# A fused two-layer kernel: the second layer's experts with the shared blocks first, biases selected by TensorE, and pairs combined behind the last block

## The reference

```
scores = softmax(x @ gate_w.T)                      # 8 experts
idx = top_k(scores + gate_b, 2);  weights = scores at idx
h1 = x @ w1.T + b1;  h3 = x @ w3.T + b3             # of an expert
a  = swiglu(h1 * h3)      # g*sigmoid(1.702 g)*(l+1), g even, l odd columns, clipped at 7
y  = a @ w2.T + b2
out = sum of weights * y over the token's 2 experts + the same for one shared expert
```

## Time and profile before

| | |
|---|---|
| median of 3 runs | 1788.88 us (1788.12 to 1789.9) |
| the profiled execution | 1786.69 us, span 1784.9 us |
| busy in the span | PE 1429.1, DVE 1327.3, ACT 909.5, POOL 617.2 us |
| in 1603.8 to 1730.7 us (routed blocks) | PE 122.66, DVE 111.14, ACT 88.70 of 126.90 us |

### The profile page before, as it was taken

The page is one execution under the profiler, slowest core; times in us unless marked ns, Lnnn a source line. Parts: engine busy times, 40 slices in busy tenths (PEclk is TensorE's granted clock), DMA queues, the critical chain, the costliest instruction groups (busy, mean ns, idle before and its releaser), DMA issues. The chain is left out here.

```text
span 1784.9 us, 41566 instructions
## 1 busy us (share of the span) xinstructions
PE 1429.1 (80%) x15014; PEld 979.8 (55%) x15014; DVE 1327.3 (74%) x3609; ACT 909.5 (51%) x2099; POOL 617.2 (35%) x586
## 2 busy tenths in 40 slices
PE   1267767776749758999999999999999983779990
PEld 0167767766744324555555555555555553658870
DVE  5699999999577855666676666667667667658886
ACT  1455555555321023666666666666666651336760
POOL 3396667665012232611111111111111003275346
PEclk7678888888859969999999999999999996689995
DMA  1310000000000001211111111111111000028962
GB/s 72 98 38 2 1 1 1 1 1 1 7 6 1 10 10 20 42 27 26 26 29 31 30 30 31 30 31 29 29 31 32 8 10 14 11 95 229 249 176 88
DMA packets 146373, 71.53 MB, mean 40 GB/s; under 512 B 95219, under 2 KB 131589, under 8 KB 146053
## 3 DMA queue, kind: packets, MB, share of 16 engines
q1 hardware_dynamic: 141508, 60.62, 15.3%
q0 software_dynamic: 4096, 8.40, 1.6%
q10 hardware_dynamic: 576, 0.07, 0.0%
HBM read 38.11 MB, written 18.35 MB: 32 GB/s over the span
## 5 line engine op out<-in xcount | busy, mean ns | idle before, releaser
L1178 DVE TENSOR_REDUCE ntop<-score 128x1 f32<-128x512 f32 x512 | 318.0, 683 | 253.0 <-PE score L1059 253.0
L1137 ACT ACTIVATE prob<-score,ntop 128x512 f32<-128x512 f32 x512 | 317.6, 687 | 270.1 <-DVE ntop L1178 270.1
L391 ACT ACTIVATE hist<-zp 128x168 f32<-128x168 f32 (+1 forms) x768 | 224.1, 313 | 171.3 <-DVE zp L359 170.6
L1095 PE MATMUL turned<-ident,prob 128*128 128x128 f32 x2048 | 268.6, 280 | 1.4 <-DVE probT L1121 1.4
L441 PEld LDWEIGHTS py<-hist,diagC 128*128 128x128 f32 x2048 | 260.3, 212 | 0.0
L441 PE MATMUL py<-hist,diagC 128*128 128x128 f32 x2048 | 260.0, 295 | 0.0
L1059 PE MATMUL score<-ks,qs 64*128 64x512 f32 x1024 | 257.2, 621 | 0.0
L1095 PEld LDWEIGHTS turned<-ident,prob 128*128 128x128 f32 x2048 | 218.9, 141 | 49.2 <-issue 28.5
L411 POOL TENSOR_TENSOR xb<-xc,Bm 128x1024 f32<-128x1024 f32 x128 | 244.7, 1948 | 1.3
L354 DVE TENSOR_TENSOR gp<-hist,Ap 128x168 f32<-128x168 f32 (+1 forms) x768 | 231.0, 331 | 14.6 <-POOL xb L411 14.6
L359 DVE TENSOR_TENSOR zp<-gp,xb 128x168 f32<-128x168 f32 (+1 forms) x768 | 234.7, 336 | 0.0
(11 more groups left out here) (293 smaller groups left out, 1571.6 us busy)
## 6 DMA issues: line engine op xcount, KB each, us to landing
w<-in_ew SPq DMA_DIRECT2D x46, 320.0 KB, 3.8
tb<-in_table SPq DMA_DIRECT2D x64, 127.1 KB
sorted_h<-nought SPq DMA_DIRECT2D x2, 2944.0 KB, 17.1
xs<-sorted_h SPq DMA_DIRECT2D x46, 128.0 KB
sorted_y<-ysb SPq DMA_DIRECT2D x46, 128.0 KB
rel_q<-q_sb SPq DMA_DIRECT2D x256, 8.0 KB
ks<-k_sb SPq DMA_DIRECT2D x32, 128.0 KB
key_q<-q_sb SPq DMA_DIRECT2D x248, 8.0 KB
```

Source lines behind the costliest of these rows:

```text
L391: nc.scalar.activation(hist[:, par, u, lo:hi], zp[j][:, 0:hi - lo], ACT.Tanh)\
L1095: last = nc.tensor.transpose(turned_ps[BANK[e]][:, j * P:(j + 1) * P], prob[G % 2][e][:, j * P:(j + 1) * P], ident[:, :])
L1137: nc.scalar.activation(prob[G % 2][e][:, :], score_ps[r][:, :], ACT.Exp, bias=ntop[:, G % 2, e:e + 1]).then_inc(prob_ready, 1)
L1178: v.tensor_reduce(ntop[:, G % 2, e:e + 1], score_ps[r][:, :], AX.X, ALU.max, negate=True)\
```

## The change

- All 16 shared blocks stand ahead of the 46 routed ones.
- SyncE's list: five weight loads and four row loads first; then for each block m the weights of m+5, the store of m, the rows of m+4.
- TensorE picks the first biases (`select`: four small products of `b1_rows` with `mine`, a one-hot table of block and expert, at step 2); ScalarE copies them out of PSUM.
- The product with b2 leaves `down`. It moves behind the last block, where TensorE adds for each tile b2's product and both gathered results, which ScalarE has multiplied by their weights; DVE adds the sum to `acc`. The eight combinations inside the loop go.
- The positions are counted in quarters of eight tiles, with three doubling steps and two additions; `tri` and the order of its product change to match. Gathers have four semaphores in turn, not eight.

```
-PARTS = 2
-PT = NT // PARTS
 SLOTS = 2 * P
 HALVES = SLOTS // P
 NSHARED = NB * SEQ // SLOTS
-RB = 2 * PT * P // SLOTS + NE1 - 1
-NROUTED = PARTS * RB
-MOST = PT * P // SLOTS
+
+QT = 8
+QUARTERS = NT // QT
+PART_QUARTERS = (2, 2)
+PARTS = len(PART_QUARTERS)
+PT = [QT * q for q in PART_QUARTERS]
+T0 = [sum(PT[:s]) for s in range(PARTS + 1)]
+RB = [2 * t * P // SLOTS + NE1 - 1 for t in PT]
+R0 = [sum(RB[:s]) for s in range(PARTS + 1)]
+NROUTED = R0[PARTS]
+MOST = max(PT) * P // SLOTS
+PART_OF = [s for s in range(PARTS) for _ in range(RB[s])]
...
-    NW, NX, NY, NGOT = 5, 4, 4, 8
+    NW, NX, NY, NGOT = 5, 4, 4, 4
     N = NSHARED + NROUTED
-    AFTER = NW
-    SHARED_FIRST, SELECT_AT, IN_LOOP, EVERY = 11, 4, 8, 2
-    ORDER = ([("shared", i) for i in range(SHARED_FIRST)] + [("routed", m) for m in range(NROUTED)]
-             + [("shared", i) for i in range(SHARED_FIRST, NSHARED)])
+    SHARED_FIRST, SHARED_THEN = 16, 0
+    SELECT_AT = 2
+    shared = lambda lo, hi: [("shared", i) for i in range(lo, hi)]
+    routed = lambda lo, hi: [("routed", m) for m in range(lo, hi)]
+    ORDER = (shared(0, SHARED_FIRST) + routed(0, RB[0]) + shared(SHARED_FIRST, SHARED_FIRST + SHARED_THEN)
+             + routed(RB[0], NROUTED) + shared(SHARED_FIRST + SHARED_THEN, NSHARED))
...
-        ball = sb("b1_all", [P, NALL, 4])
-        bsel = sb("b1_sel", [P, NROUTED, 4])
-        bprod = sb("b1_prod", [P, NROUTED, 4, NE1])
+        b1_shared = sb("b1_shared", [P, 4])
+        b1_rows = sb("b1_rows", [NE1, 4 * P])
+        b1_sel = sb("b1_sel", [P, 4, NROUTED])
+        owni = sb("owni", [P, 1], I32)
+        own = sb("own", [P, 1])
+        mine = sb("mine", [NE1, NROUTED])
...
-            load_slots(0)
+                sp.dma_start(rows(ys, m), ysb[m % NY][:, :, :]).then_inc(y_out[m % NY], 16)
+
+            for m in range(NW):
+                load_weights(m)
+            for m in range(NX):
+                load_slots(m)
             for m in range(NROUTED):
-                if m + 1 < NROUTED:
-                    load_slots(m + 1)
-                load_weights(m)
-                if m >= AFTER:
-                    store(m - AFTER)
-            for m in range(NROUTED - AFTER, NROUTED):
+                if m + NW < NROUTED:
+                    load_weights(m + NW)
                 store(m)
+                if m + NX < NROUTED:
+                    load_slots(m + NX)
...
+                    if n == SELECT_AT + 1:
+                        act.wait_ge(spots_ps, 2)
+                        A.copy(b1_sel[:, :, :].rearrange("p c m -> p (c m)"), XT[0][:, 0:4 * NROUTED])\
+                         .then_inc(sel_ready, 1)
                     if n == SHARED_FIRST:
-                        act.wait_ge(eid_ready, 2)
+                        act.wait_ge(sel_ready, 1)
                     gate(n)
...
+            for k in range(NT):
+                act.wait_ge(got_in[k % NGOT], 32 * ring(k, NGOT))
+                for r in range(2):
+                    A.activation(got[:, 2 * k + r, :], got[:, 2 * k + r, :], ACT.Copy, scale=wt[:, r, k:k + 1])\
+                     .then_inc(weighted, 1)
...
+                for q in range(T0[s] // QT + 1, T0[s + 1] // QT):
+                    chain.add(v.tensor_tensor(src[:, q, :, :], src[:, q, :, :],
+                                              src[:, q - 1, QT - 1:QT, :].to_broadcast([P, QT, NE1]), ALU.add))
+            chain.wait()
+            v.sem_inc(chosen_ready, 1)
...
+            v.tensor_scalar(mine[:, :], eidf[0:NE1, :], own[0:NE1, 0:1], None, ALU.is_equal).then_inc(eid_ready, 1)
...
-            def combine(k):
-                dve.wait_ge(got_in[k % NGOT], 32 * ring(k, NGOT))
-                for r in range(2):
-                    v.scalar_tensor_tensor(acc[:, k, :], got[:, 2 * k + r, :], wt[:, r, k:k + 1], acc[:, k, :],
-                                           ALU.mult, ALU.add).then_inc(combined, 1)
-                    dve.wait_ge(combined, 2 * k + r + 1)
-
             def finish(j):
+
                 ts = slice(j * TPB, (j + 1) * TPB)
+                dve.wait_ge(summed, j + 1)
+                chain(v.tensor_tensor(acc[:, ts, :], acc[:, ts, :],
+                                      pm[SUMS_IN[j]][:, :].rearrange("p (q e) -> p q e", q=TPB), ALU.add))
...
-                    if kind == "shared":
-                        k = i * HALVES + o
-                        mm(Y[n % 2][:, cols], cwT[:, k * P:(k + 1) * P], b2[:, :], start=True, stop=False)
-                    last = mm(Y[n % 2][:, cols], a[:, n % 2, cols], w[:, 4 * P:5 * P],
-                              start=(kind == "routed"), stop=True)
+                    last = mm(Y[n % 2][:, cols], a[:, n % 2, cols], w[:, 4 * P:5 * P], start=True, stop=True)
                 last.then_inc(y_ready, 1)
 
+            def select():
+
+                pe.wait_ge(eid_ready, 2)
+                for c in range(4):
+                    last = mm(XT[0][:, c * NROUTED:(c + 1) * NROUTED],
+                              b1_rows[:, :].rearrange("e (p c) -> e c p", c=4)[:, c, :], mine[:, :],
+                              start=True, stop=True)
+                last.then_inc(spots_ps, 1)
+
             for n in range(N + 2):
+                if n == SELECT_AT:
+                    select()
+                if n + 1 == SHARED_FIRST:
+                    pe.wait_ge(sel_ready, 1)
                 if n + 1 < N and ORDER[n + 1][0] == "routed":
                     turn(ORDER[n + 1][1])
                 if n < N:
                     up(n)
                 if n >= 2:
                     down(n - 2)
+            for j in range(NBLK):
+                if SUMS_IN[j] == 6:
+                    pe.wait_ge(y_taken, N)
+                for q in range(TPB):
+                    k = j * TPB + q
+                    bank = pm[SUMS_IN[j]][:, q * P:(q + 1) * P]
+                    mm(bank, cwT[:, k * P:(k + 1) * P], b2[:, :], start=True, stop=False)
+                    for r in range(2):
+                        pe.wait_ge(weighted, 2 * k + r + 1)
+                        last = mm(bank, ident[:, :], got[:, 2 * k + r, :], start=False, stop=(r == 1))
+                last.then_inc(summed, 1)
```

More of the change, by code:

```diff
@@ L1296, in experts1 @@
         fulls = sb("fulls", [P, MOST])
-        numberi = sb("numberi", [P, RB], I32)
-        number = sb("number", [P, RB])
+        numberi = sb("numberi", [P, max(RB)], I32)
+        number = sb("number", [P, max(RB)])
         expi = sb("expi", [P, NE1], I32)
@@ L1305, in experts1 @@
         chosen = sb("chosen", [P, NT, NE1])
-        upto = [sb(f"upto{i}", [P, PARTS, PT + 1, NE1]) for i in range(2)]
+        upto = [sb(f"upto{i}", [P, QUARTERS, QT, NE1]) for i in range(2)]
         top = sb("top1", [P, NT])
@@ L1424, in _ @@
             for s in range(PARTS):
-                for k in range(s * PT, (s + 1) * PT):
+                for k in range(T0[s], T0[s + 1]):
                     for r in range(2):
@@ L1430, in _ @@
                 for i in range(NY):
-                    pool.wait_ge(y_out[i], 16 * stores(i, (s + 1) * RB))
-                for k in range(s * PT, (s + 1) * PT):
+                    pool.wait_ge(y_out[i], 16 * stores(i, R0[s + 1]))
+                for k in range(T0[s], T0[s + 1]):
                     if k >= NGOT:
@@ L1504, in _ @@
             norm.vector(dve, chain)
-            dve.wait_ge(w_in, 16 * 4)
+            dve.wait_ge(w_in, 16 * 5)
             dve.wait_ge(consts, CONSTS)
             for dst, src in ((rank[:, :], ranki[:, :]), (expn[:, :], expi[:, :]), (fulls[:, :], fullsi[:, :]),
-                             (number[:, :], numberi[:, :])):
+                             (number[:, :], numberi[:, :]), (own[:, :], owni[:, :])):
                 chain.add(v.tensor_copy(dst, src))
@@ L1524, in _ @@
             dve.wait_ge(chosen_ready, 1)
-            src = chosen[:, :, :].rearrange("p (s k) e -> p s k e", s=PARTS)
+            src = chosen[:, :, :].rearrange("p (q k) e -> p q k e", q=QUARTERS)
             for i in range(STEPS):
-                by, dst = 1 << i, upto[(i + 1) % 2][:, :, 1:PT + 1, :]
+                by, dst = 1 << i, upto[i % 2][:, :, :, :]
                 chain.add(v.tensor_copy(dst[:, :, 0:by, :], src[:, :, 0:by, :]))
-                chain(v.tensor_tensor(dst[:, :, by:PT, :], src[:, :, by:PT, :], src[:, :, 0:PT - by, :], ALU.add))
+                chain(v.tensor_tensor(dst[:, :, by:QT, :], src[:, :, by:QT, :], src[:, :, 0:QT - by, :], ALU.add))
                 src = dst
-            v.sem_inc(chosen_ready, STEPS)
+            for s in range(PARTS):
+                for q in range(T0[s] // QT + 1, T0[s + 1] // QT):
[3 more added lines that the diff above has]
+            v.sem_inc(chosen_ready, 1)
             chain.add(v.tensor_tensor(cw[:, :, 0:NE1], chosen[:, :, :], probs[:, :, :], ALU.mult))
@@ L1553, in _ @@
             for s in range(PARTS):
-                chain.add(v.tensor_tensor(spot[:, s * PT:(s + 1) * PT, :], spots[:, s, 0:PT, :],
```

(10 more changed lines are left out.)

112 lines of the change are left out of this document (46 added, 66 removed).

## The result

The changed kernel takes 2086.6 us (median of 4 runs, 2085.1 to 2087.4), the kernel before 1788.5 us beside it (4 runs, 1786.7 to 1789.9): a ratio of 1.167, 95% interval 1.1655 to 1.1685. The forecast was 2093 us. The profiled execution has a span of 2084.8 us, 299.9 more than before.

A forecast was written before the change was run, and what follows sets the result against it. The last stage was taken as the bound: a line of scatter, routed blocks, gathers and tail. 1786.7 + 303.1 (blocks) + 1.5 (tail) = 2091.3, with 2.2 for the median 2093 us; range 1985 to 2135.

The forecast's parts named there:

- 42 waits: In the routed blocks, TensorE stands still before turns 4 to 45 until their sorted rows land: 42 times.
- Wait, 5.4 us: TensorE's idle from a routed `down` to the landing of the next turn's rows: 5.4 us, between 4.1 and 6.6.
- Part (a): First piece of one wait: from the end of `down` to SyncE's issue of the weight load, 1.0 us.
- Part (b): Second piece of one wait: from the weight load's issue to the row load's landing, 4.4 us.
- Own work, 4.5 us: TensorE's own part of a routed round: 4.5 us, between 4.1 if the clock rises each time and 4.9 if never.
- Start: Start of the routed blocks: turn 0 stays at 1598.3 us, first routed `down` ends at 1610.7 instead of 1613.2.
- Last three `down`s: End of the routed blocks: `down(43)` to `down(45)` follow the 42 rounds in about 7.3 us.
- Tail, +1.5 us: Behind the last gather's landing: weightings, last product and three DVE operations take 3.7 us instead of 2.2, +1.5 us.
- rival 1: SyncE's queue order costs nothing, TensorE finds rows landed: 1782 us, chance 0.04.
- Rival 2: TensorE's clock stays at 2.4 GHz in the routed rounds: 7.84 us a round, 2007 us, chance 0.14.
- Rival 3: Row loads aren't held up by the weight load and store ahead: 8.6 us a round, 2038 us, chance 0.17.
- Rival 4: Queue slower than taken and clock never rises: up to 11.5 us a round, 2160 us, likely middle 2135, chance 0.12.

The follow-up runs named there:

- e1: The changed kernel with SyncE's list back in the order of the kernel before: 1792.1 us, ratio 1.002.
- e2: The kernel before with SyncE's new list alone: 2077.4 us, ratio 1.1627.
- e3: The changed kernel with six buffers for sorted rows in place of four: 1796.7 us, ratio 1.0034.
- e6b: e1 with the product with b2 back in the shared blocks' `down`, 13 shared blocks first and 3 last: 1786.5 us, ratio 0.998.
- e8: e1 with the gathered results of four tiles summed in two products of 512 columns in place of eight of 128: 1783.2 us, ratio 0.9966.
- e4: The changed kernel with ten unread products behind each routed `down`: 1995.0 us, ratio 1.114.
- e10: The changed kernel with SyncE's loop in the order store, row load, weight load: 2004.8 us, ratio 1.1212.
- e9: e8 with tokens sorted and gathered in three parts, 12 shared blocks first and 4 between the first two routed stretches: 1780.9 us, ratio 0.9952.
- e11: e9 with the last group of four tiles summed tile by tile in narrow products: 1780.6 us, ratio 0.9957.

## Why the prediction was right

Its mechanism stood: the row load of a block is behind the store of a block whose `down` is TensorE's last work ahead of that row's `turn`. e1 and e2 put the loss on that list, and e3 shows that the distance in it decides: the landing took as long there and cost next to nothing. By its steps:

- **42 waits**: 42 of the 43. Right.
- **Wait, 5.4 us**: 205.1/42 = 4.88. Part (a), 1.0 us from `down` to the weight load's issue, was 0.72. The difference is about that of SyncE's register load, which took 0.27 us in the median here and 0.58 before (0.71 in the earlier trace rows); why it was slower before stays open. Part (b), 4.4 us from there to the row's landing, was 4.06: close to the 3.73 of the store in the earlier trace rows and far from the 5.6 bound.
- **Own work, 4.5 us**: 199.6/42 = 4.75. I had half of the rounds rising to 2.4 GHz before their end; about a third did (0.63 granted over the 42 rounds). A wait shorter by 0.5 and work longer by 0.25 leave a round of 9.64 instead of 9.9: 42 x 0.26 = 11 us of the sum.
- **Start**: turn 0 at 1597.3 (1598.3 expected), first routed `down` at 1609.9 (1610.7). Right: five more shared blocks and TensorE's selection fit ahead of the first rows, with 7.9 us to spare where I had 5.
- **Last three `down`s**: 6.0 us, 7.3 expected.
- **Tail, +1.5 us: the mis-sized term.** It was +13.7. I set 96 products of 0.41 us beside 41 us of gathers and left the low clock to the range. TensorE went at 1.2 GHz from 2023 us on: 32 tiles x 1.87 us = 60 us, so it and not GpSimd's gathers sets the end, which e6b and e8 confirm: they take the products with b2 away or make the sums wide, and gain 5.7 and 8.9 us over e1.
- **Behind the last add**: -3.7 us, not foreseen.
- **Rivals**: rival 1 (the order costs nothing) fell by e1 and e2. Rival 2 (clock at 2.4 GHz) is e4, where it was forced: 7.29 us a round, 7.84 expected. Rival 3 (rows not held up) has an answer in e10: behind a weight load and a store a row takes 3.2 us, behind the store alone 2.2. So it was right of the store and wrong of the weight load, while I had put both ahead of X. Rival 4's 1.2 GHz came true in most rounds, its slower queue did not.

The sum came out only 6 us too high by luck, because the errors had both signs: -13 us in the blocks (2033.8 expected, 2020.6 measured), +12.2 and -3.7 behind them, the rest in the medians.

## What to carry to other kernels

In a queue that runs in order, count in rounds of the consuming engine the distance from a store that must wait to the load issued behind it, and compare it with the distance from the store's producer to the load's user: where they were equal here, each round paid the full latency. Two more buffers gave 290 of the 298 us back, and the load's move one round forward 231. Such a wait also lowered TensorE's clock: 97 us of the loss was the round's own work at half speed. Work moved behind the last block must be priced at the clock that TensorE has there: here 60 us for the 32 tiles, and not 39.

## What the runs showed of the hardware that I had not expected

TensorE was busy for all of 56.00 us in the tail and its granted clock stayed at 0.50, in the changed kernel and in e1. Idle time is thus not needed to stay at 1.2 GHz. With products of 512 columns in the same place the clock was at 0.50 in e8 from 1729 to 1739 us, with TensorE busy from 1729.61 on, and then at 1.00. But narrow products alone don't keep it low either: in e6b, which has the products of 128 columns with `got` and none with b2 between them, it rose at 1741.8 us, 4 us after they began (1737.83), and TensorE did 65 of their passes in the 8 us from 1742 at 1.00. So it is the mix of both kinds that ran at 0.50 throughout; which property of it counts is not shown. Unread products that fill a wait sped up a kernel by 92 us.

The end of the span isn't the end of the last add. The kernel before, e6b, e9 and e11 have their last gather issued at 1774.08, 1772.28, 1766.89 and 1767.04 us and end 10.8, 10.9, 12.1 and 12.1 us later, while the last add ends 6.1, 4.5, 2.9 and 5.8 us ahead of the end; in the changed kernel, whose DVE comes late, the span ends 2.4 us behind the last add and 21.9 us behind the last gather. What takes the 11 to 12 us behind the last gather stays open: no experiment took GpSimd's list apart. It is probably the reason why e11 gained nothing, why e6b gained half of what was expected, and why the -3.7 us above came about.
